# Key and value blocks of three batches filled by transfers within the chip's memory

## What is computed

```python
q = (layernorm(x) @ w_q.T + b_q).reshape(B, Nq, 16, 16).transpose(0, 2, 1, 3)     # B = 4, Nq = 1024
kv = (ctx @ w_kv.T + b_kv).reshape(B, 77, 16, 32).transpose(0, 2, 1, 3)
k, v = kv[..., :16], kv[..., 16:]
attn = softmax(einsum('bhqd,bhkd->bhqk', q, k) / sqrt(16))
x = x + einsum('bhqk,bhkd->bhqd', attn, v) -> (B, Nq, 256) @ w_out.T + b_out
# then x = x + moe_ffn(layernorm(x)): top-2 of 8 experts, 1024 hidden units each
```

## Time and profile before

| | us |
|---|---|
| three runs | 767.00, 769.16, 766.27 |
| median | 767.0 |
| span of the profiled execution | 769.2 |
| PE busy in it | 680.1 |
| DVE busy | 564.4 |
| POOL busy | 430.1 |
| ACT busy | 406.3 |

### The profile page before, as it was taken

One profiled execution on the slowest core, in us unless ns is written; L12 is line 12 of the kernel. 1 busy time (PEld: TensorE's weight loads), 2 busy tenths in 40 slices (PEclk: granted clock), 3 DMA queues, 4 the chain that ended last, 5 costly groups with the idle time before them and its releaser, 6 DMA issues.

```text
span 769.2 us, 15696 instructions
## 1 busy us (share of the span) xinstructions
PE 680.1 (88%) x5592; PEld 649.1 (84%) x5592; DVE 564.4 (73%) x1198; ACT 406.3 (53%) x955; POOL 430.1 (56%) x547
## 2 busy tenths in 40 slices
PE   5999999999999834999999999999999999999500
PEld 4789999998988723999999999999999999999500
DVE  5589898988888797665565679777696666854187
ACT  3356555555555594454454467455464454643185
POOL 6744665565564334436445558766576554632456
PEclk9699999999999955999999999999999999999855
DMA  9501101011010122434344446544455343322484
GB/s 295 176 15 43 42 28 43 30 41 43 29 43 29 42 85 65 149 84 94 51 107 69 81 106 123 125 96 73 98 123 114 46 101 52 58 29 28 64 266 150
DMA packets 55764, 64.10 MB, mean 83 GB/s; under 512 B 9472, under 2 KB 50944, under 8 KB 55552
## 3 DMA queue, kind: packets, MB, share of 16 engines
q0 software_dynamic: 15360, 21.31, 17.1%
q1 hardware_dynamic: 39616, 41.64, 16.6%
q10 hardware_dynamic: 704, 0.01, 0.0%
HBM read 39.22 MB, written 23.72 MB: 82 GB/s over the span
## 4 chain that ended last, share of the span: by engine, by line
PE 81%; DVE 11%; issue 3%; DMA 2%; ACT 1%; POOL 1%; POOLq 0%; SPq 0%; DVEq 0%; ACTq 0%
PE banks L897 18%; PE banks L899 18%; PE banks L898 18%; PE banks L1039 8%; PE banks L1025 5%; PE banks L1013 5%; PE banks L1171 2%; PE banks L1075 1%; PE banks L920 1%; DVE oh_lo L1485 1%; PE banks L942 1%; DVE oh_id L1481 1%; DVE z L1741 1%; DMA res<-sum_rows 1%; DVE z L1735 1%
## 5 line engine op out<-in xcount | busy, mean ns | idle before, releaser
L611 POOL DMA_INDIRECT sum_rows<-y_sb,slot_ids x80 | 131.4, 1643 | 162.1 <-ACT y_sb L840 145.4
L850 ACT ACTIVATE hraw<-banks,b_now 128x256 f32<-128x256 f32 x320 | 132.2, 477 | 90.3 <-PE banks L899 80.5
L897 PE MATMUL banks<-xT_hi,w_hi 128*128 128x256 f32 x560 | 161.6, 289 | 1.7 <-ACT xT_hi L822 1.7
L899 PE MATMUL banks<-xT_hi,w_lo 128*128 128x256 f32 x560 | 158.5, 283 | 0.0
L898 PE MATMUL banks<-xT_lo,w_hi 128*128 128x256 f32 x560 | 158.4, 283 | 0.0
L897 PE MATMUL banks<-w_hi,h_hi 128*128 128x256 f32 x528 | 148.8, 282 | 1.3 <-issue 1.3
L898 PE MATMUL banks<-w_lo,h_hi 128*128 128x256 f32 x528 | 148.6, 281 | 0.0
L899 PE MATMUL banks<-w_hi,h_lo 128*128 128x256 f32 x528 | 148.5, 281 | 0.0
L1701 DVE TENSOR_TENSOR h_lo<-hraw,h_hi 128x512 fp32r<-128x512 f32 x160 | 114.6, 716 | 5.5
L1699 DVE CAST h_hi<-hraw 128x512 fp32r<-128x512 f32 x160 | 77.5, 485 | 45.8 <-ACT hraw L850 44.6
L897 PEld LDWEIGHTS banks<-xT_hi,w_hi 128*128 128x128 f32 x560 | 106.3, 190 | 2.2 <-issue 2.1
(11 more groups left out here) (216 smaller groups left out, 1442.7 us busy)
## 6 DMA issues: line engine op xcount, KB each, us to landing
w1raw<-in_w1T SPq DMA_DIRECT2D x8, 1024.0 KB
w2raw<-in_w SPq DMA_DIRECT2D x8, 1024.0 KB
xn_rows<-xn SPq DMA_DIRECT2D x32, 128.0 KB, 1.8
sum_rows<-xn SPq DMA_DIRECT2D x32, 128.0 KB, 1.8
out<-z SPq DMA_DIRECT2D x16, 256.0 KB, 2.2
res<-sum_rows SPq DMA_DIRECT2D x7, 512.0 KB, 8.5
X<-in_x SPq DMA_DIRECT2D x2, 1280.0 KB, 12.1
xg<-xn_rows,slot_ids POOLq DMA_INDIRECT x80
```

What stands on the lines that cost most here:

```text
L611: g.indirect_dma_start(sum_rows, bass.IndirectOffsetOnAxis(ap=slot_ids[:, st, 1, q:q + 1], axis=0), y_sb[:, u, q, :], None, bounds_check=N ...
L850: a.activation(hraw[:, j // 2, j % 2, :], banks[:, j // 2, (j % 2) * 256:(j % 2 + 1) * 256], ACT.Silu, bias=b1_now[:, (c // SPE) % 2, j:j ...
L897: t_.matmul(o, a_hi, b_hi, start=first, stop=False)
L899: return t_.matmul(o, a_lo, b_hi, start=False, stop=last)
```

## The change

Batches 1 to 3 no longer have their blocks computed. POOL writes zeros over that part of `KH_hi`, `KH_lo` and `VB` in three large memsets. Then SP copies the non-zero parts into place: 16 transfers for the keys (each 16 partitions, 6 pieces of 77 numbers in each), and 12 for the values (15 to 77 partitions, 6 pieces of 16 numbers in each). They come in SP's queue ahead of the first stores of `xn2`, and the transfers of the keys also ahead of the zeros, gamma and beta. PE waits for all key transfers before step 8 and for all value transfers and the column of ones before step 9. The layout of `kT_hi` and `kT_lo` changes so that a transfer's source is one block per partition. `v_hi` and `v_lo` shrink to batch 0. The six later copies of the column of ones move behind the memsets. DVE's wait for the last loads of X moves from after step 1 into step 1.

```diff
+        def rows_of_head(h):
+
+            first, end = h * NK, (h + 1) * NK
+            for j in range(NJ):
+                a, b = max(first, JS * j + (1 if j else 0)), min(end, JS * j + JW)
+                if a < b:
+                    yield j, a - JS * j, a - first, b - a
...
+            sp.wait_ge(sem("kT_made"), DC)
+            sp.wait_ge(sem("kT_split"), DC)
+            sp.wait_ge(sem("blocks_cleared"), 2)
+            for blocks, keys in ((KH_hi, kT_hi), (KH_lo, kT_lo)):
+                blocks = blocks[:].bitcast(f32).rearrange("p (g h k) -> p g h k", h=HH, k=NK)
+                keys = keys[:].bitcast(f32).rearrange("p b f k -> p (b f) k")
+                for h in range(HH):
+                    rows = slice(h * DH, (h + 1) * DH)
+                    sp.dma_start(blocks[rows, 2:, h, :], keys[rows, 2:, :]).then_inc(keys_spread, 16)
             sp.wait_ge(sem("zero_made"), 1)
...
             sp.dma_start(beta_sb[:], row(beta)).then_inc(load_gb, 16)
+            sp.wait_ge(sem("v_made"), NB)
+            sp.wait_ge(sem("blocks_cleared"), 3)
+            columns = VB[:].rearrange("r (g j w) -> r g j w", j=NJ, w=VW)
+            values = v_sb[:].rearrange("k b (f w) -> k (b f) w", f=2)
+            for h in range(HH):
+                for j, r, k, n in rows_of_head(h):
+                    sp.dma_start(columns[r:r + n, 2:, j, h * DW:h * DW + DH],
+                                 values[k:k + n, 2:, h * DH:(h + 1) * DH]).then_inc(values_spread, 16)
...
-            for bf in range(2 * NB):
+            def ones_column(bf):
...
+            for bf in range(2):
+                ones_column(bf)
...
             rstd_first(0)
+            g.memset(KH_hi[:, 2 * KH:].bitcast(f32), 0.0).then_inc(sem("blocks_cleared"), 1)
             spread_lo(0)
             rstd_first(1)
...
-            for b in range(1, NB):
-                spread_lo(b)
+            g.memset(KH_lo[:, 2 * KH:].bitcast(f32), 0.0).then_inc(sem("blocks_cleared"), 1)
+            g.memset(VB[:, 2 * NJ * VW:], 0.0).then_inc(sem("blocks_cleared"), 1)
+            pool.wait_ge(sem("blocks_cleared"), 3)
+            for bf in range(2, 2 * NB):
+                ones_column(bf)
...
-            def later_values(b):
-                if b == 2:
-                    act.wait_ge(sem("v_made"), NB)
-                    a.activation(v_hi[:, 1:NB, :], v_sb[:, 1:NB, :], ACT.Copy).then_inc(sem("v_hi_made"), 1)
...
+                if t == TPB:
+                    pe.wait_ge(keys_spread, 16 * KEY_MOVES)
+                if t == TPB + 1:
+                    pe.wait_ge(sem("v_ones_made"), 2 * NB)
+                    pe.wait_ge(values_spread, 16 * VALUE_MOVES)
...
-                if values_of_step(t) is not None:
-                    n, js = values_of_step(t)
-                    pe.wait_ge(sem("shifted"), 2 * t + 1)
-                    for j in js:
-                        spread(n, j, banks[0:JW, LB, (j % 2) * D:(j % 2 + 1) * D])
...
-                if keys_of_step(t) is not None:
-                    spread_keys(*keys_of_step(t))
...
-                if values_of_step(t) is not None:
-                    n, js = values_of_step(t)
-                    dve.wait_ge(sem("v_rows_done"), n * NJ + js[-1] + 1)
-                    for j in js:
-                        spread_values(n, j, banks[0:JW, LB, (j % 2) * D:(j % 2 + 1) * D])
...
-            def spread_rest(b):
-                if b == 2:
-                    values_lo(1, NB - 1, 2)
-                    for n in (2, 3):
-                        dve.wait_ge(load_x[n], 16)
```

More of the change, by code:

```diff
@@ L267, in xattn_moe_kernel, with attention_steps @@
         stored = dma_sem("stored")
+        keys_spread, values_spread = dma_sem("keys_spread"), dma_sem("values_spread")
         block = root.enter_context(nc.Block())
-        def attention_steps(engine, step, spread=None):
+        def attention_steps(engine, step):
             for i in range(PAIRS + 1):
@@ L276, in attention_steps @@
                     step(i, u)
-                    if spread is not None and 2 * i + u < NB - 1:
-                        spread(2 * i + u + 1)
             step(PAIRS + 1, 0)
@@ L706, in _ @@
             act.wait_ge(sem("v_made"), 1)
-            a.activation(v_hi[:, 0, :], v_sb[:, 0, :], ACT.Copy).then_inc(sem("v_hi_made"), 1)
+            a.activation(v_hi[:], v_sb[:, 0, :], ACT.Copy).then_inc(sem("v_hi_made"), 1)
             def router_parts(j, bank):
@@ L1537, in step @@
                     first_values(4)
+                    for n in (2, 3):
+                        dve.wait_ge(load_x[n], 16)
                     dve.wait_ge(sem("w_hi_ready"), 2)
```

70 lines of the change are left out of this document (27 added, 43 removed).

## The result

The changed kernel takes 770.1 us (median of 5 runs, 768.6 to 770.8) against 767.0 (765.5 to 769.2) for the kernel before on the same chip: ratio 1.0038, 95% interval 1.0025 to 1.0052. That is 3.1 us slower, where 5.0 us faster was forecast, and it lies above the range.

The account below looks back on a forecast made before the run. PE was taken as the bound from 47 to 217 us, with waits for DVE and a DVE/POOL chain before. Terms 3.4 + 1.1 + 0.5 = 5.0 us off the median 767.0 gave 762.0 us, range 759.8 to 766.6.

Parts of the forecast that it names:

- hidden: Prologue, KH_hi memset between rstd and the first KH_lo product: 3.3 us within POOL's 5.13 us of idling, so no cost.
- The first rival: Prologue: var does not get in between the two late memsets, PE's scores come 3.3 us late, 765.3 us; chance 0.17.
- 21.64: Time in us when the earlier kernel's second var ended, having got through amid POOL's KH_lo products.
- The clock, left as it is: Prologue: time at the lower clock left unchanged; a longer time there than now was a sign of being wrong.
- The 30 products: Attention steps with row pieces: 30 products removed from PE save 3.4 us, ends 2.3 and 3.6.
- Step 2: Without v_hi and v_lo ahead of this step, vals is ready earlier for PE: 1.1 us, ends 0.95 and 1.6.
- The copies: Start of the kernel: six copies moved away, var runs unhindered, the chain starts 0.5 us earlier; ends 0 and 0.55.
- DVE's and ACT's work in the steady steps: DVE loses some 1.4 us in a step like step 5 but had time to spare: gain 0.
- The transfers: SP issues each in about 0.33 us, keys by 28 and values by about 38, before PE needs them: cost 0.
- SP issuing values for over 10 us: Sign of being wrong, in SP's queue; the forecast had 12 value transfers issued by about 38 us.
- the second rival: Value pieces clog few DMA engines, the xn2 store sticks, POOL cannot write in step 4: 803 us; chance 0.10.
- The third rival: Prologue gives nothing back, a load or ACT being late next; products give 2.3, in all 3.3, 763.7 us; chance 0.15.

Follow-up runs that it names:

- both waits: Changed kernel, POOL's KH_hi memset waiting for xn of tiles 0 and 1, its two late memsets for the third var: 763.8 us, ratio 0.9949.
- new forms: Changed kernel, memsets unmoved, DVE's xn written as scalar_tensor_tensor and var as tensor_tensor instead of tensor_scalar: 763.7 us, ratio 0.9951.
- first wait alone: Changed kernel, POOL zeroing KH_hi only when xn of tiles 0 and 1 is made, late memsets unmoved: 766.6 us, ratio 0.9987.
- six pieces: Changed kernel, the memset of KH_hi cut into six of 616 columns back to back, no wait added: 769.7 us, ratio 1.003.
- the kernel with the products put back: Changed kernel with POOL's memsets waiting for xn and the third var, plus the 30 products back on PE, without DVE's work: 765.0 us, ratio 0.9967.

## Why the prediction failed, step by step

Where each kernel is, by the starts of PE's scores (us; third profile of the kernel before, since it has no fall of the clock in step 22):

| | before | changed | both waits | new forms |
|---|---|---|---|---|
| lower clock level before it, lasts | 10.2 | 17.1 | 13.7 | 10.2 |
| start of step 2 | 38.14 | 44.74 | 38.66 | 38.00 |
| step 2 | 7.78 | 6.20 | 6.21 | 6.20 |
| steps 3 to 20 | 132.35 | 129.97 | 129.93 | 129.91 |
| steps 21 to 24 | 28.87 | 28.88 | 28.89 | 28.87 |
| from there to the end | 558.7 | 558.1 | 558.0 | 559.3 |
| span | 765.8 | 767.9 | 761.7 | 762.3 |

**The memsets: wrong, and nearly all of the miss.** The step that failed first is "hidden", said of the memset of `KH_hi` because POOL idles for 5.13 us there. POOL's own stream had the room, and `KH_lo` wasn't late. But this memset follows `rstd` in POOL's queue, and DVE's `xn` waits for `rstd`, so the two start within 0.2 us of each other, and `xn` was the instruction that PE waited for the earlier trace rows. The prediction weighed DVE against the late memsets and never against this one. Price: 3.0 us at step 2; 3.9 us by the medians (1.0038 less 0.9987), intervals of some 1 us each.

The second failed step is the one that it named and took at 0: that `var` gets through at the end of the first late memset. The first rival did happen, `var` took 5.19 us, and the price was the foretold one: 3.1 us at step 2, against 3.3. What spoke for the rival were the close copies at the start, what spoke against it was 21.64. The first was nearer to the memsets, because these too stand back to back with no wait in the code, and each `KH_lo` product has one ahead of it. It was no sure sign, though: in two of five profiles the copies let `var` in.

Together they take 6.1 us at step 2, and 6.8 by the medians (1.0038 less 0.9949). Without them the forecast of 762.0 would have met 763.1 to 763.2 (767.0 times 0.9949 and 0.9951), 1.1 to 1.2 us above it and within the range. The rest of the miss is in the terms below.

**The clock, left as it is: it moved.** This was one of its signs of being wrong. In the changed kernel the lower level lasts from 20.1 to 37.2, with both waits from 17.1 to 30.8, that is 3.4 us less, and in the kernel before 13.7, 10.2 and 10.2 us. The stretch of the changed kernel is shown above; this is the one with both waits:

```profile
17.00:30.00 13.00, 13.00 (x56) 10.83 (x56) 9.40 (x21) 2.97 (x9) 11.09 (x22) 0.51 0.85 275
```

In the changed kernel the gap in which PE waited for `xn1T_lo` lies within the low stretch (PE is busy for 14.42 of 17 us), here PE has no gap in it. The level lasts 17 us in the three kernels in which `var` is shut out for 5.19 us (changed, first wait alone, six pieces), and 10.2 to 13.7 in all others, so the longer stretch goes with that stall. I can't separate the two. Some of it is scatter: the kernel with the products put back has the same prologue as the one with both waits, stays at the lower level for 10.2 us and begins step 2 at 37.47, 1.2 earlier. Against that profile the changed kernel is 7.3 us late at step 2, against the one in the table 6.1. The 6.8 by the medians lies between.

**The 30 products: right mechanism, term too large.** 2.4 to 2.5 us measured, 3.4 taken, 2.3 the lower end. The step that failed is the choice between two rows: the pitch says what PE spends, step 25 said what the stream gets back, and I leaned to the pitch. "PE stays the bound" was not quite so. What was late next was ACT's `probsT`.

**Step 2: gain larger than taken.** 1.58 us, 1.1 taken, 1.6 the upper end. 1.09 of it is the split, just what I had taken; 0.09 the moved waits, which I had not priced; 0.4 open.

**The copies:** 0.3 to 0.5 us in POOL's rows, 0.5 taken, unresolved in the total. The reason given was only part of it: `var` was not held in every execution, and the larger part was POOL's own queue.

**DVE's and ACT's work in the steady steps, 0: right.** With the products back and without DVE's part, steps 3 to 20 take 132.40.

**The transfers, 0: right in sum, wrong in price.** SP's queue in the changed kernel:

```profile
25.07 6.29 SPq L404 DMA_DIRECT2D KH_hi<-kT_hi  x8
31.40 5.08 SPq L404 DMA_DIRECT2D KH_lo<-kT_lo  x8
...
38.72 13.96 SPq L416 DMA_DIRECT2D VB<-v_sb  x12
53.60 0.34 SPq L423 DMA_DIRECT2D xn_rows<-xn  x1
```

One key transfer costs SP 0.7 us and one value transfer 1.2, not the 0.33 of a store. The values are issued by 52.7 and not by 38. The first store of `xn2` goes at 53.60 instead of 49.87, but not because of them: POOL makes that buffer at 53.57, late by the stalls of the prologue. With both waits it is made at 47.49, and there the store does stand behind the values, whose issue ends at 50.61. It goes at 50.65, 3.2 us late, and nothing waits for it. My sign "SP issuing values for over 10 us" came up, and meant nothing: PE never waits for `keys_spread` or `values_spread`, and POOL's step 4 waits for no store. From 56 to 58 us the DMA engines are idle, so the pieces had landed well before the 66 us of the second rival:

```profile
56.00:58.00 2.00, 2.00 (x20) 1.94 (x18) 1.49 (x4) 1.14 (x4) 1.84 (x5) 1.00 0.00 0
```

That rival (803 us) did not happen. Whether few engines carried the values, as the rule of the Trainium skill on divisors ("DMA: Bandwidth & Descriptors", section "Why a DMA increments its semaphore by 16 and not by 1") would have it, no row here shows. The third rival's size for the products was right, its reason (the start gives nothing back) was not what happened.

**Sum of the gains.** 2.4 + 1.6 + 0.3 to 0.5 = 4.3 to 4.5 us, against 3.9 measured without the collisions (interval 2.9 to 5.0), and 5.0 forecast.

The best kernel here is the changed one with both collisions gone, or the second down to 1.77 us: 763.5 to 764.0 us in four variants (ratios 0.9943 to 0.9957), all within each other's intervals, and 0.5% below the kernel before. Waits on POOL and other forms on DVE do equally well.

## What to carry to other kernels

Work put into an engine's idle time is hidden only if nothing that runs beside it on another engine needs what it holds: for each memset, copy or multiplication of GpSimd look at what VectorE runs in that stretch, and whether both start behind the same instruction. If something must stay there, write VectorE's instruction as a tensor_tensor or scalar_tensor_tensor, which helped under memsets and not under multiplications, or move the memset behind it by a semaphore. Cutting it into six pieces did not help; a wait between two memsets did. And when work leaves the bounding engine, price it by a like step without it, not by its pitch: the difference is the next wait.

## What was unexpected of the hardware

- Between memsets the lock goes from POOL to DVE only where POOL waits. Five boundaries within 3.37 us of memsets let nothing in, a gap of 0.05 us did. Multiplications with a wait ahead that was already met let DVE in at the next boundary, and copies with none let it in in two of five profiles. The page of the Trainium skill named above speaks of a whole instruction; here it was a whole row of them, 5.19 us for `var`.
- The form of `xn` that is shut out is worth little where nothing is in its way: 0.74 us for two, against 0.91 as scalar_tensor_tensor.
- An idle gap of PE can be paid twice: 1.7 us of waiting, then 1.4 us more in step 3, at a clock of 0.57 from 47 to 51 us. But the clock also fell for 3.4 us, at a price of 1.5, with no gap ahead, in one profile of a kernel and not in the next.
- A transfer that scatters small pieces holds SP for 0.6 to 2.5 us at its issue, where the store of a whole tile of `xn2` takes 0.34.
